# Convolution and attention in one kernel: z statistics from PSUM, moved products of Wo, one-image pieces, a later relu

## The reference

```
# layer 0: a non-local block. z is normalised over batch and pixels, by channel
theta = conv1x1(x, theta_w, theta_b); phi, g = maxpool2(conv1x1(x, ...))
y = softmax(theta^T phi / sqrt(128)) g
z = conv1x1(y, wz_w, wz_b)
z = (z - mean(z)) / sqrt(var(z) + 1e-5) * bn_gamma + bn_beta      # statistics of the batch itself
x = x + z
# layer 1: convolutions with weights rounded to powers of two, activations rounded to 16 bits
quant(x): scale = max(max|x|, 1e-12) / 32767; round(x / scale) * scale   # max over the whole tensor
h = conv1x1(quant(x), w1)                       # 256 -> 64
h = relu(bn1(depthwise3x3(quant(h), peg) + peg_b))
h = relu(bn2(conv3x3(quant(h), w2)))
x = relu(bn3(conv1x1(quant(h), w3)) + x)        # 64 -> 256
# layer 2 and 3, on tokens (8 x 256, 256 channels), each with layer norm and residual
t += attention(ln(t)); t += ln(t) @ ternary(weight)^T
t += attention(ln(t)); t += Wo (sum of the two best of 8 experts of ln(t))
```

## Time and profile before

| | |
|---|---|
| three executions | 673.96, 676.16, 677.71 us; median 676.16 |
| the profiled execution | 677.57 us, its span 674.5 |
| PE, PEld busy | 600.4 (89%), 409.3 (61%) us |
| VectorE, ScalarE, GpSimd busy | 447.7 (66%), 332.9 (49%), 117.9 (17%) us |
| first block ends | about 120.6 us |
| granted TensorE clock, mean | 0.956 |

### The profile page before, as it was taken

The page is one execution under the profiler, slowest core; times in us unless marked ns, Lnnn a source line. Parts: engine busy times, 40 slices in busy tenths (PEclk is TensorE's granted clock), DMA queues, the critical chain, the costliest instruction groups (busy, mean ns, idle before and its releaser), DMA issues.

```text
span 674.5 us, 11227 instructions
## 1 busy us (share of the span) xinstructions
PE 600.4 (89%) x4159; PEld 409.3 (61%) x4206; DVE 447.7 (66%) x1274; ACT 332.9 (49%) x556; POOL 117.9 (17%) x115
## 2 busy tenths in 40 slices
PE   6877775667899999999999988999999999999897
PEld 2746223554677677677677776666575756565443
DVE  4677757736575785775775775675858667675464
ACT  2377556624665665665655655344343525253110
POOL 2021000142133133132032132002020200000000
PEclk9998786797899999999999998999999999999999
DMA  9400000299863763774673671707145170000000
GB/s 339 203 0 1 0 0 0 39 154 145 121 122 65 105 119 71 102 123 84 81 128 76 80 131 34 118 1 137 21 94 63 40 118 17 2 16 1 17 7 24
DMA packets 40253, 50.64 MB, mean 75 GB/s; under 512 B 4052, under 2 KB 33492, under 8 KB 39892
## 3 DMA queue, kind: packets, MB, share of 16 engines
q1 hardware_dynamic: 40200, 49.94, 39.5%
HBM read 35.11 MB, written 14.68 MB: 74 GB/s over the span
## 4 chain that ended last, share of the span: by engine, by line
PE 58%; DVE 14%; DMA 4%; issue 3%; ACT 2%; SPq 1%; POOL 0%; DVEq 0%; ACTq 0%
PE ps L1247 14%; PE ps L1130 8%; PE ps L1122 7%; PE ps L1204 5%; PE ps L1193 4%; DVE nmax L1414 4%; PE ps L1114 4%; PE ps L1189 3%; PE ps L1173 3%; PE ps L1165 3%; PE ps L1211 2%; DVE acc L1494 2%; PE ps L1168 2%; DVE xn L1370 2%; DVE stats L1359 2%
## 5 line engine op out<-in xcount | busy, mean ns | idle before, releaser
L1414 DVE TENSOR_REDUCE nmax<-ps 128x2 f32<-128x512 f32 (+1 forms) x192 | 130.9, 687 | 79.2 <-PE ps L1173 51.2
L1307 ACT ACTIVATE PT<-ps 128x512 f32<-128x512 f32 x192 | 113.4, 597 | 116.8 <-PE ps L1193 115.1
L1247 PE MATMUL ps<-wm,xnT 128*128 128x512 f32 x256 | 119.9, 599 | 0.7
L1074 POOL TENSOR_TENSOR rstd<-ve,fix 128x2 f32<-128x2 f32 x32 | 22.2, 695 | 328.4 <-DVE ve L1365 328.4
L1301 ACT ACTIVATE QS<-ps 8x1024 bf16<-8x1024 f32 x64 | 65.1, 1017 | 26.5 <-PE ps L1178 24.5
L1193 PE MATMUL ps<-QS,KS 110*128 110x256 bf16 (+3 forms) x512 | 74.9, 248 | 0.0
L1494 DVE SCALAR_TENSOR_TENSOR acc<-ps,gate,acc 128x256 f32<-128x256 f32 x128 | 61.6, 481 | 18.5 <-PE ps L1247 16.2
L1247 PEld LDWEIGHTS ps<-wm,xnT 128*128 128x128 f32 x256 | 45.1, 190 | 39.7 <-issue 38.1
L1122 PE MATMUL ps<-xnT,by_dim 128*128 128x256 f32 x256 | 63.3, 394 | 2.2 <-ACT xnT L1272 2.2
L1094 POOL TENSOR_TENSOR parts<-rest,fix 128x512 bf16<-128x512 f32 x30 | 38.1, 1269 | 143.1 <-DVE rest L1383 99.1
L1189 PE MATMUL ps<-fixb 128*128 128x256 bf16 (+1 forms) x192 | 60.1, 313 | 2.3 <-DVE nmax L1414 2.0
(11 more groups left out here) (210 smaller groups left out, 938.3 us busy)
## 6 DMA issues: line engine op xcount, KB each, us to landing
parts_dram<-parts SPq DMA_DIRECT2D x32, 384.0 KB, 3.3
QS<-parts_dram SPq DMA_DIRECT2D x96, 128.0 KB
KS<-parts_dram SPq DMA_DIRECT2D x96, 128.0 KB, 7.7
wt<-wt_dram SPq DMA_DIRECT2D x1, 2562.0 KB, 18.9
wm<-wm_dram SPq DMA_DIRECT2D x1, 2449.0 KB, 13.2
xc<-x_dram SPq DMA_DIRECT2D x8, 256.0 KB, 5.4
out_dram<-res SPq DMA_DIRECT2D x8, 256.0 KB, 2.1
w<-w_dram SPq DMA_DIRECT2D x1, 845.0 KB, 7.8
```

Of the source, the lines that this page charges most:

```text
L1247: mm = pe.matmul(d, normT(stage, batch)[:, c, t * P:(t + 1) * P], M("We", c * EXPERTS * CH + e * 2 * CH, 2 * CH), start=(c == 0), stop=(c ...
L1307: act.activation(PT[:, pt_slot(piece, n), :], bank(piece), ACT.Exp).then_inc(drain(piece), 1)
L1414: dve.tensor_reduce(group[:, 0, :] if part == 0 else group[:, 1, 2 * part - 2:2 * part], bank(piece).rearrange("p (j n) -> p j n", n=w_), ...
```

## The change

Nothing is changed in what is computed, nor in the second block.

- `z_to_sbuf` goes. VectorE's statistics read the bank itself, without the bias, and `scale_z` reads the bank too; `affine_z` makes up for the bias with two steps more (`z_t`), ahead of its wait on GpSimd, and one step less behind it.
- The three steps on the ternary weight go into VectorE's loop of maxima of k = 2, behind the first.
- PE's and ScalarE's order of the experts: turns 3 to 5 as before; then `all_max(0, 1)`, folds 3 and 4, turn 6, w1's product; behind `all_max(1, 2)` fold 6 and turn 7; behind `all_max(2, 3)` fold 7 and be's turn; behind `all_max(3, 4)` fold 5 and be's product. ScalarE writes out folds 3, 4 and turn 6 behind the roundings of k = 0, fold 6 and turn 7 behind those of k = 1, fold 7 and be's turn behind those of k = 2, fold 5 and be behind those of k = 3. Other banks are used, so there are new waits of PE on `folded` and `fold_turned_out` in the rounds.
- `scale_ready` is raised as soon as `isc` (k = 0, 2, 3) or `fac` (k = 1) is there; `facn` follows with a semaphore of its own, for which ScalarE waits ahead of its first `n1`. For k = 0 it is not made.
- The rounds k = 1 and 2 run in six pieces, `RUNS`: images 0; 1; 2 and 3; 4 and 5; 6; 7.
- bn3's bias is added to x1 by ScalarE in place, a quarter after each of the first four relus of rounds 1 and 2. `pre` then needs no bias; PE transposes `pre` itself, and ScalarE takes the relu in the copy to `X`, all eight of them; VectorE copies none.

The diff, cut to its core (indented by eight less):

```diff
+RUNS = ((0, 1), (1, 1), (2, 2), (4, 2), (6, 1), (7, 1))
+RUN_BANKS = ((4, 5, 6, 7, 0, 1), (0, 1, 2, 3, 6, 7))
...
-    TURN_BANK = (2, 3, 4, 6, 7, 0, 6, 3)
-    FOLD_BANK = (5, 2, 0, 1, 2, 4, 5, 6)
-    BE_TURN_BANK, BE_FOLD_BANK = 4, 5
+    TURN_BANK = (2, 3, 4, 0, 6, 1, 6, 7)
+    FOLD_BANK = (5, 2, 0, 4, 5, 3, 6, 4)
+    FOLD_ORDER = (0, 1, 2, 3, 4, 6, 7, 5)
+    BE_TURN_BANK, BE_FOLD_BANK = 5, 2
...
         for e in range(3, 6):
-            pe.wait_ge(z_out, e - 2)
+            pe.wait_ge(z_scaled, e - 2)
             turn_expert(e)
-        pe.wait_ge(z_out, 4)
+        pe.wait_ge(z_scaled, 8)
+        all_max(0, 1)
         fold_expert(3)
-        pe.wait_ge(z_out, 5)
         fold_expert(4)
-        pe.wait_ge(z_out, 8)
+        pe.wait_ge(fold_turned_out, 5)
         turn_expert(6)
-        turn_expert(7)
-        fold_expert(5)
-        fold_expert(6)
-        all_max(0, 1)
-        fold_expert(7)
-        pe.wait_ge(folded, 6)
-        for c in range(NC2):
-            mm = pe.transpose(ps[:, BE_TURN_BANK, c * EXPERTS:(c + 1) * EXPERTS],
-                              M("be", c * P, P)[0:EXPERTS, :], F("ident")[0:EXPERTS, 0:EXPERTS])
-        mm.then_inc(fold_turned, 1)
...
-                           M("Wo", c * CH, CH), start=(c == 0), stop=(c == 1))
-        mm.then_inc(fold_done, 1)
         all_max(1, 2)
-        pe.wait_ge(folded, 9)
+        pe.wait_ge(folded, 4)
+        fold_expert(6)
+        pe.wait_ge(scale_ready, 2)
+        turn_expert(7)
         for k, (src, wgt) in enumerate(((hp1, dwq), (hp2, w2q))):
-            for q in range(4):
-                pe.wait_ge(parts_ready, 4 + 4 * k + q + 1)
+            for r, (image, images) in enumerate(RUNS):
+                pe.wait_ge(parts_ready, 4 + len(RUNS) * k + r + 1)
+                if k == 0:
+                    pe.wait_ge(folded, min(4 + r, 6))
+                    pe.wait_ge(fold_turned_out, 8 if r >= 3 else 7)
                 for tap in range(9):
                     dy, dx = divmod(tap, 3)
-                    mm = pe.matmul(ps[:, 4 * (1 - k) + q, :], wgt[:, tap, :],
-                                   src[:, 2 * q:2 * q + 2, dy:dy + IMG, dx:dx + IMG],
+                    mm = pe.matmul(ps[:, RUN_BANKS[k][r], 0:images * PIX], wgt[:, tap, :],
+                                   src[:, image:image + images, dy:dy + IMG, dx:dx + IMG],
                                    start=(tap == 0), stop=(tap == 8))
                 mm.then_inc(conv_done, 1)
             all_max(2 + k, 3 + k)
+            if k == 0:
+                fold_expert(7)
+                for c in range(NC2):
+                    mm = pe.transpose(ps[:, BE_TURN_BANK, c * EXPERTS:(c + 1) * EXPERTS],
+                                      M("be", c * P, P)[0:EXPERTS, :], F("ident")[0:EXPERTS, 0:EXPERTS])
+                mm.then_inc(fold_turned, 1)
+            else:
+                fold_expert(5)
+                pe.wait_ge(fold_turned_out, 9)
+                for c in range(NC2):
+                    mm = pe.matmul(ps[0:EXPERTS, BE_FOLD_BANK, 0:CH], turned_be[:, c * EXPERTS:(c + 1) * EXPERTS],
+                                   M("Wo", c * CH, CH), start=(c == 0), stop=(c == 1))
+                mm.then_inc(fold_done, 1)
         for q in range(4):
-            pe.wait_ge(parts_ready, 12 + q + 1)
+            pe.wait_ge(parts_ready, 4 + 2 * len(RUNS) + q + 1)
             for o in range(NC2):
                 n = 2 * q + o
+                if n == 0:
+                    pe.wait_ge(folded, 7)
+                if n == 6:
+                    pe.wait_ge(folded, 9)
                 pe.matmul(ps[:, (4 + n) % 8, :], w3q[:, o * P:(o + 1) * P], hq3[:, q * QUART:(q + 1) * QUART],
                           start=True, stop=True).then_inc(conv_done, 1)
         for n in range(8):
-            pe.wait_ge(x2_ready, 2 * (n // 2) + 2)
...
                     mm = pe.transpose(ps[:, (4 + n) % 8, k * CH + c * P:k * CH + (c + 1) * P],
-                                      x2[:, c, t * P:(t + 1) * P], F("ident"))
...
-            act.activation(x1[:, o, sl], z[:, o, sl], ACT.Identity, scale=z_a[:, o:o + 1],
+            act.activation(x1[:, o, sl], ps[:, (6 + 4 * o + QUARTERS[n]) % 8, :], ACT.Identity, scale=z_a[:, o:o + 1],
...
+        for e in range(3, 6):
+            expert_turned(e)
...
         for k in range(1, 4):
             act.wait_ge(scale_ready, k + 1)
-            for q in range(4):
-                sl = slice(q * QUART, (q + 1) * QUART)
-                src = ps[:, q, :] if k == 1 else h[:, sl]
+            for r in range(len(RUNS)) if k < 3 else range(4):
+                sl = run(r) if k < 3 else slice(r * QUART, (r + 1) * QUART)
+                src = h[:, sl]
+                if k == 1:
+                    q, place = in_bank(r)
+                    src = ps[:, q, place]
                 act.activation(n256[:, sl], src, ACT.Copy, bias=ROUND_256, scale=fac[k]).then_inc(rounded, 1)
+                if r == 0:
+                    act.wait_ge(facn_ready, k)
                 act.activation(n1[:, sl], src, ACT.Copy, bias=ROUND_1, scale=facn[k]).then_inc(rounded, 1)
+            if k == 1:
+                expert_folded(6)
+                expert_turned(7)
+            if k == 2:
+                expert_folded(7)
+                act.wait_ge(fold_turned, 9)
+                act.activation(turned_be, ps[:, BE_TURN_BANK, 0:NC2 * EXPERTS], ACT.Copy).then_inc(fold_turned_out, 1)
+            if k == 3:
+                expert_folded(5)
+                act.wait_ge(fold_done, 9)
+                act.activation(M("be")[0:EXPERTS, :], ps[0:EXPERTS, BE_FOLD_BANK, 0:CH], ACT.Copy).then_inc(folded, 1)
             if k < 3:
-                for q in range(4):
-                    sl = slice(q * QUART, (q + 1) * QUART)
-                    act.wait_ge(conv_done, 4 * k + q + 1)
-                    act.activation(h[:, sl], ps[:, 4 * (2 - k) + q, :], ACT.Relu, bias=bnb[k - 1],
+                for r in range(len(RUNS)):
+                    act.wait_ge(conv_done, 4 + len(RUNS) * (k - 1) + r + 1)
+                    act.activation(h[:, run(r)], ps[:, RUN_BANKS[k - 1][r], 0:RUNS[r][1] * PIX], ACT.Relu, bias=bnb[k - 1],
                                    scale=aff_a[k - 1]).then_inc(relu_out, 1)
-        for q in range(4):
-            sl = slice(q * QUART, (q + 1) * QUART)
-            for o in range(NC2):
-                act.wait_ge(res_added, 2 * q + o + 1)
-                act.activation(x2[:, o, sl], pre[:, o, sl], ACT.Relu, bias=bnb[2][:, o:o + 1]).then_inc(x2_ready, 1)
-        for n in range(0, 8, 2):
+                    if r < 4:
+                        x_ = x1[:, k - 1, r * QUART:(r + 1) * QUART]
+                        act.activation(x_, x_, ACT.Identity, bias=bnb[2][:, k - 1:k]).then_inc(x1_biased, 1)
+        for n in range(8):
             act.wait_ge(tok_done, n + 1)
             act.activation(X[:, 2 * n:2 * n + 2, :].rearrange("p a n -> p (a n)"), ps[:, (4 + n) % 8, :],
-                           ACT.Copy).then_inc(tok_out_act, 1)
+                           ACT.Relu).then_inc(tok_out, 1)
...
-        settle(dve.tensor_scalar(T("tern"), T("tern"), tern_inv, ROUND_1, ALU.mult, ALU.add))
-        settle(dve.tensor_scalar(T("tern"), T("tern"), ROUND_1, -1.0, ALU.subtract, ALU.max))
-        settle(dve.tensor_scalar(T("tern"), T("tern"), 1.0, tern_scale, ALU.min, ALU.mult))
...
+                dve.wait_ge(z_done, 4 * o + q + 1)
+                op = dve.bn_stats(zst[:, o, q, :], ps[:, (6 + 4 * o + q) % 8, :])
...
         def affine_z(o):
             c = slice(o, o + 1)
+            bias = A0("wz_b", o, 1)
+            settle(dve.tensor_tensor(z_t[:, c], zmv[:, o, 0:1], bias, ALU.add))
+            settle(dve.tensor_tensor(z_t[:, c], bias, z_t[:, c], ALU.subtract))
             dve.wait_ge(z_pow, o + 1)
             settle(dve.tensor_tensor(z_a[:, c], z_rstd[:, c], A0("gamma", o, 1), ALU.mult))
-            settle(dve.tensor_tensor(z_t[:, c], z_a[:, c], zmv[:, o, 0:1], ALU.mult))
-            dve.tensor_tensor(z_b[:, c], A0("beta", o, 1), z_t[:, c], ALU.subtract).then_inc(z_affine, 1)
+            dve.scalar_tensor_tensor(z_b[:, c], z_t[:, c], z_a[:, c], A0("beta", o, 1), ALU.mult, ALU.add)\
+               .then_inc(z_affine, 1)
...
-            settle(dve.reciprocal(isc[k], scl[k]))
             if acc_scale is not None:
-                settle(dve.tensor_tensor(fac[k], isc[k], acc_scale, ALU.mult))
-            dve.tensor_tensor(facn[k], fac[k], F("low_half"), ALU.mult).then_inc(scale_ready, 1)
+                settle(dve.reciprocal(isc[k], scl[k]))
+                dve.tensor_tensor(fac[k], isc[k], acc_scale, ALU.mult).then_inc(scale_ready, 1)
+            else:
+                dve.reciprocal(isc[k], scl[k]).then_inc(scale_ready, 1)
+            if k:
+                dve.wait_ge(scale_ready, k + 1)
+                dve.tensor_tensor(facn[k], fac[k], F("low_half"), ALU.mult).then_inc(facn_ready, 1)
         def affine_of(k):
...
+                if k == 2 and r == 0:
```

(8 more changed lines are left out.)

94 lines of the change are left out of this document (36 added, 58 removed).

## The result

| | before | changed kernel |
|---|---|---|
| median of 14 executions each | 676.16 us (673.68 to 678.88) | 672.52 us (669.6 to 674.69) |
| ratio, 95% interval | 1 | 0.9939 (0.9921 to 0.9957) |
| profiled execution, its span | 677.57, 674.5 us | 673.81, 672.0 us |
| first block, from z's first product to its end | 82.7 us | 76.9 us |
| second block, from there to the span's end | 554.2 us | 556.8 us |

The kernel is faster by 0.6%, 3.6 us between the medians; 6.2 had been forecast. Of the 3.8 us between the two profiled executions 2.5 lie in the span and 1.3 outside it (3.1 us around the span before, 1.8 after). The two lower rows of the table hold what this text is about: in this pair of profiles the first block gives 5.9 us, close to the forecast, and the second block, whose code is the same, is 2.6 us longer.

A forecast was written before the change was run, and what follows sets the result against it. The prediction saw a chain of hand-overs in the first block, no engine always busy; seven gains summed to 6.2 us, taking the median 676.2 to 670.0, own range 668.3 to 671.8, wider range 666.8 to 673.2.

The forecast's parts named there:

- rival C: Clock stays low from w1's product through round 1; 4.6 of the gain go, 674.6 us; chance 0.13.
- z: First stage: statistics from PSUM start sooner, but z_t steps block behind GpSimd's add; gain 1.3 us (0.5 to 2.3).
- folds out of all_max's way: First hand-over of the maximum: PE's expert folds no longer delay it; gain 1.7 us (1.0 to 1.9).
- facn: Made after scale_ready, its step leaves the chain four times, ahead of ScalarE's roundings; gain 0.8 us (0.6 to 0.8).
- round 1: First convolution round in six pieces, PE stalling before piece 2 for fold 6; gain 0.4 us (-2 to +2.1).
- round 2: Second convolution round in six pieces, its end set by ScalarE's queue; gain 0.8 us (0.4 to 2.4).
- shorter last maxima: Last maximum of each convolution round covers 256 columns instead of 512; gain 0.5 us for both.
- end: First block's tail: PE turns the last pair at once without the relu between; gain 0.7 us (0.2 to 0.9).
- second block: Work unchanged, so a microsecond off the chain is one off the kernel, save its first microseconds; change 0.
- outside the span: Time around the profiled span, 3.1 us, kept as it was in the forecast; change 0.
- rival D: Lower clock all through, moved folds directly ahead of the convolutions; 17.2 us lost against 6.2 won, 687.0; chance 0.04.
- rival A: ScalarE is not last in the second convolution round, PE's end rules; 668.4 us; chance 0.11.

The follow-up runs named there:

- one_input: Changed kernel with z's four small affine steps on VectorE given one tensor input and a per-partition scalar each: 671.13 us, ratio 0.9926 to the kernel before.
- bias_early: Changed kernel with x1's bias steps moved out of the rounds' relus, six ahead of round 1 and two behind its last relu: 669.68 us, ratio 0.9905.
- banks_and_bias: Changed kernel with both edits, other banks for round 1's pieces and x1's bias steps moved out of the relus: 669.56 us, ratio 0.9902.
- first_after: Changed kernel without its second block, the first block's tokens stored instead: 125.03 us, against 130.47 for the kernel before cut likewise.
- other_banks: Changed kernel with round 1's pieces 2 and 3 in banks 0 and 1, so only pieces 4 and 5 wait for fold 6: 671.40 us, ratio 0.9915.
- two_image_pieces: Changed kernel with four pieces of two images in each convolution round instead of six pieces: 669.55 us, ratio 0.9893.
- The fillers: Unused TensorE products added ahead of two layer-norm waits in the second block: 676.28 us in the kernel before, 672.39 in the changed kernel.

## Why the prediction came out as it did

It fell into the range of 666.8 to 673.2 and on the right side, with 0.6 of the forecast gain. But 672.5 lies outside the forecast's own 668.3 to 671.8; the room beyond it was made for the unknown steps' bounds and for a part of rival C, the clock low from w1's product through round 1, and neither is what used it up. That the wider range held is in part luck. By its own steps, from z's first product on, in the profiles:

| term | forecast | measured |
|---|---|---|
| z | 1.3 | 1.45 |
| folds out of all_max's way | 1.7 | 1.5, less 0.3 in the second hand-over |
| facn | 0.8 | 0.8 |
| round 1 | 0.4 | 0.1 |
| round 2 | 0.8 | 0.9 |
| shorter last maxima | 0.5 | 0.5 |
| end | 0.7 | 0.9 |
| first block | 6.2 | 5.9 |
| second block | 0 | -2.6 in this pair |
| start of z's first product | 0 | -0.75 in this pair |
| outside the span | 0 | 1.3 in this pair |

The last column gives 3.8, the difference of the two profiled executions. The first block's sum is close also because small misses of both signs cancel. A slip of the forecast's own is in rival D, whose terms make 687.2 and not 687.0.

**z.** Right with its mechanism: the first `z_t` step fell into GpSimd's second add and lasted 1.11. That one_input takes this away shows it.

**The hand-over.** Right in kind. What was too small is the lower clock's price for the small product: 0.95 of idle time for the 0.78 that the forecast makes (0.58 and 0.2). The second hand-over, which the sum left as it was, loses 0.3 in the same way.

**Round 1.** The stall before piece 2 was forecast at 2.1 us and ended by ScalarE's copy to wm; it was 1.58 and ended so. But piece 0 began 2.1 us after the first rounding instead of 1.6, since fold 6 (3.20) stood ahead of it at the lower clock. The forecast's reason for the upper clock there (no hole, since PE runs the fold in it) did not hold for the fold itself. In ten profiles of the changed kernel and its variants the fold took 3.1 to 3.5 in seven and 1.89 in three (bias_early, banks_and_bias, first_after), by the clock ahead of z's first product. And in round 1, too, ScalarE's queue was nearer to the end than counted: without the stall it is last, as other_banks shows, so that covering the stall, for which the forecast's bound had 2.1, gave only 0.9.

**Round 2.** Right: ScalarE's queue sets the end; rival A, PE last, came true only in variants: those that take x1's steps out of the queue, and two_image_pieces, which has fewer steps in the queue.

**The pieces as such.** The sum made them a gain of 1.2 in the rounds, with another 0.5 in the maxima, against the kernel before. Part of this was not theirs: with two-image pieces the rounds already fall to 11.2, because the fold and the turn moved ahead of the products close PE's hole. The comparison with the nearest other form of the change, rather than with the kernel before alone, would have shown it from the same numbers: 1.6 to 2.2 to the first product, 8.1 of products, 0.8 of relu is 10.5 to 11.1, less than the 12.5 and 12.0 forecast for six pieces.

**The second block.** This is the term that failed, put at nothing. "The work there is unchanged; a microsecond off the chain is one off the kernel, save that the second part's first microseconds depend on transfers and on TensorE's clock" is right for the work, but the clock matters beyond the first microseconds. The earlier trace rows gives it as 1.00 over 490 us, and I took that for no dip; but 3.4 us at the lower level take only 0.003 off such a mean. Low stretches of 0 to 10 us in all, worth 0 to 4.5 us, are in these profiles, close to the whole forecast gain. By the medians of many executions the loss is smaller than in the first pair: 5.4 (first blocks by themselves) against 3.6 to 4.6 for whole kernels, so 1 to 2 us. Of this 0.7 are the small jumps, which are there in every profile of the changed kernel and which the forecast's "a microsecond off the chain is one off the kernel" excludes; their cause is open. Of the 2.6 us between the first two profiles, 1.3 are the longer dip at the second place, 0.7 the small jumps and 0.6 the first 55 us. That the changed kernel draws the dips more often is not shown: all three profiles of the kernel before had at most a short dip at the second place, and one of them a dip at the first; of nine of the changed family seven had the first and six the long one at the second, and one_input, of the same family, had none. The executions without a profile don't show where their dips were, but their mean clocks speak against it: over 54 and 20 executions the second block's time at the lower level came out the same within some 3 us, where these nine and three profiles differ by 4.5 at the two places. The fillers that were to settle it missed the gaps, so this rests on averages alone.

**Outside the span.** The forecast took the 3.1 us of the one profiled execution for a constant. Over the same 54 and 20 executions it was 2.3 before (1.8 to 3.0) and 1.8 after (1.7 to 1.9): 0.5 us of the measured gain lies there, for a reason that no run shows. In spans the mean gain is 3.9, in times 4.3.

## What to carry to other kernels

Where a queue in strict order sets a stage's end, smaller pieces only pay once their added instructions and the bank that they wait for are out of that queue's way; work out the plain form of the same change beside it before you choose. Compare variants only where the clock was the same in the steps compared, or take what it cost out first. Look for the lower clock in short stretches (here 8 and 12 us) around each short idle time of TensorE, before and after: an average of 1.00 over hundreds of microseconds hides several us. And a gain in one part of a kernel is best timed with that part alone as well as in the whole.

## What the runs showed of the hardware

- After the same two idle times of TensorE (0.86 and 1.24 us, or 1.1 and 1.9) in otherwise dense work, the granted clock stayed at 1.00 in some executions; in others it was 0.79 over 8 us, which is 3.4 us at the lower level, or 0.72 over 12 us at the second place, which is 6.7. The price was 1.4 to 1.6 us for the short dip and 2.6 to 2.9 for the long one.
- A one-column VectorE step with two SBUF tensor inputs lasted 1.11 us beside a GpSimd add, and 0.20 with the second input as a per-partition scalar. Away from GpSimd the forms cost 0.14 to 0.22 and 0.20 to 0.27.
- On ScalarE, relus of 256 columns out of PSUM last 0.56 and of 512 columns 0.78, and two of 256 back to back take 1.02: a split piece costs this queue 0.24 more than a whole one.
- TensorE did 54 mixed products of 256 and 512 columns in 8.31 to 8.51 us and the same columns as 36 products of 512 in 8.27: the split costs it up to 0.2.
- Code that is the same word for word took 0.7 us longer behind a changed first block, in jumps at fixed places, in eight profiles of eight; at one of them VectorE stood idle for 0.48 to 0.50 us between two of its own steps, in none of the four other profiles.
